# First attention and FFN of a two-layer transformer in one stage, the FFN six tiles behind

## The reference

```python
x = x + _L0_xattn_ref(_layernorm(x), ctx, ctx, Wq, bq, Wk, bk, Wv, bv, Wo, bo)   # 8 heads of 64, softmax over 64
x = x + _L0_ffn_ref(_layernorm(x), w_gate, w_up, w_down, s_gate, s_up, s_down)   # 512 -> 1376 -> 512
x = x + _L1_xattn_ref(_layernorm(x), ctx, ctx, ...)                              # linear attention
x = x + _L1_ffn_ref(_layernorm(x), W, b, A, Bmat, LiMEs)                         # low-rank experts
...
def int4_quant(x):
    beta = jnp.mean(jnp.abs(x), axis=-1, keepdims=True)
    return jnp.clip(jnp.round(x * SQRT7 / (beta + EPS)), -8, 7) * beta
def _L0_ffn_ref(x, w_gate, w_up, w_down, s_gate, s_up, s_down):
    xq = int4_quant(x)
    gate = jnp.square(jax.nn.relu(bitlinear(xq, w_gate, s_gate)))    # weights rounded to -1, 0, 1
    return bitlinear(int8_quant(bitlinear(xq, w_up, s_up) * gate), w_down, s_down)
```

## Time and profile before

| | us |
|---|---|
| median of 3 runs (757.1 to 757.83) | 757.25 |
| the profiled execution | 760.02 |
| its span, first to last instruction | 758.2 |
| busy in the span: PE | 683.5 (90%) |
| DVE | 610.3 (80%) |
| ACT | 489.1 (65%) |
| POOL | 383.5 (51%) |

### The profile page before, as it was taken

One profiled execution on the slowest core, in us unless ns is written; L12 is line 12 of the kernel. 1 busy time (PEld: TensorE's weight loads), 2 busy tenths in 40 slices (PEclk: granted clock), 3 DMA queues, 4 the chain that ended last, 5 costly groups with the idle time before them and its releaser, 6 DMA issues. The chain is left out here.

```text
span 758.2 us, 17720 instructions
## 1 busy us (share of the span) xinstructions
PE 683.5 (90%) x6622; PEld 351.3 (46%) x6649; DVE 610.3 (80%) x971; ACT 489.1 (65%) x884; POOL 383.5 (51%) x331
## 2 busy tenths in 40 slices
PE   6999999999978767599999869999999999958997
PEld 2455445454546555444444324444444444424643
DVE  6878788978745667579999868999999999958355
ACT  3888867676715666577677617878878878754320
POOL 2000009999944676432212317768777687634224
PEclk9999999999998999799999969999999999997899
DMA  5234555556334223014333200000000000025405
GB/s 169 66 127 138 201 183 146 141 155 172 82 83 130 65 68 81 10 35 78 78 69 63 65 19 1 1 2 1 1 2 1 1 2 1 1 42 109 73 1 222
DMA packets 92600, 54.71 MB, mean 72 GB/s; under 512 B 76964, under 2 KB 76964, under 8 KB 92516
## 3 DMA queue, kind: packets, MB, share of 16 engines
q1 hardware_dynamic: 91764, 53.06, 26.7%
q10 hardware_dynamic: 752, 0.52, 0.2%
HBM read 32.00 MB, written 4.19 MB: 48 GB/s over the span
## 5 line engine op out<-in xcount | busy, mean ns | idle before, releaser
L1432 POOL TENSOR_TENSOR query_qn<-query_eq,query_rq 128x1024 f32<-128x1024 f32 x64 | 122.0, 1906 | 53.3 <-DVE query_rq L1366 51.3
L684 ACT ACTIVATE keys_ek<-keys_psK,keys_mk 128x512 f32<-128x512 f32 x128 | 86.9, 684 | 40.0 <-DVE keys_mk L536 38.2
L536 DVE TENSOR_REDUCE keys_mk<-keys_psK 128x2 f32<-128x1024 f32 x64 | 78.0, 1218 | 17.2 <-PE keys_psK L743 16.9
L1357 DVE TENSOR_REDUCE query_mq<-query_psQ 128x16 bf16<-128x1024 f32 x64 | 75.5, 1180 | 4.9 <-PE query_psQ L1520 4.7
L1451 ACT ACTIVATE query_eq<-query_psQ 128x1024 f32<-128x1024 f32 x64 | 65.2, 1019 | 21.5 <-PE query_psQ L1533 21.5
L1363 DVE TENSOR_REDUCE query_lq<-query_eq 128x16 f32<-128x1024 f32 x64 | 77.3, 1207 | 2.2 <-ACT query_eq L1451 2.1
L1542 PE MATMUL query_psX<-all_ident,query_qn 128*128 128x128 f32 x512 | 70.7, 282 | 0.4 <-ACT query_qT L1458 0.4
L754 PE MATMUL keys_psT<-all_ident,keys_ek 128*128 128x128 f32 x512 | 70.8, 282 | 0.0
L766 PE MATMUL keys_psG<-keys_eT,keys_cT 128*64 128x512 f32 x256 | 69.0, 617 | 1.0 <-issue 0.9
L754 PEld LDWEIGHTS keys_psT<-all_ident,keys_ek 128*128 128x128 f32 x512 | 55.5, 142 | 28.2 <-issue 20.0
L1458 ACT ACTIVATE query_qT<-query_psX 128x1024 f32<-128x1024 f32 x64 | 65.4, 1022 | 1.1 <-PE query_psX L1542 1.1
(11 more groups left out here) (270 smaller groups left out, 1442.2 us busy)
## 6 DMA issues: line engine op xcount, KB each, us to landing
all_ring<-in_L_ffn_w_down_dram SPq DMA_DIRECT2D x8, 688.0 KB, 4.6
all_ring<-in_L_ffn_w_gate_dram SPq DMA_DIRECT2D x10, 512.0 KB, 5.4
all_ring<-in_L_ffn_w_up_dram SPq DMA_DIRECT2D x10, 512.0 KB, 4.0
all_x_res<-in_x_dram SPq DMA_DIRECT2D x4, 1024.0 KB, 6.2
att_ctx_n<-in_ctx_dram SPq DMA_DIRECT2D x16, 256.0 KB, 3.1
out_dram<-all_x_res SPq DMA_DIRECT2D x16, 256.0 KB, 2.1
all_cf<-in_ctx_dram SPq DMA_DIRECT2D x15, 256.0 KB, 2.7
att_w_nat<-in_L_ffn_W_dram SPq DMA_DIRECT2D x4, 256.0 KB, 4.4
```

The source lines that it names most:

```text
L536: dve.tensor_reduce(mk[:, c, :], psK[c % 2][:, :, :], X, ALU.max, negate=True).then_inc(mk_ok, 1)
L684: act.activation(ek[t % 2][b][:, c, :], psK[c % 2][:, b, :], ACT.Exp, bias=mk[:, c, b:b + 1], accum_out=le[t % 2][:, b, c:c + 1]).then_inc ...
L1357: dve.tensor_reduce(mq[g % 2][:, :, 0:HEADS], psQ[g % 2][:, :, :].rearrange("p b (h d) -> p b h d", d=D), X, ALU.max, negate=True).then_in ...
L1432: pool.tensor_tensor(qn[m % 2][:, :, :], eq[m % 3][:, :, :], rq[m % 2][:, :].unsqueeze(2).broadcast_to([P, 2 * HEADS, D]), ALU.mult).then_ ...
```

## The change

`attention0` and `feed_forward` become one function, `attention_and_ffn`, in one block with 25 steps. Step i handles attention tile i and FFN tile j = i - 6 (LAG), so steps 0 to 5 only attend, 6 to 15 do both, step 16 finishes tile 15 and feeds tile 10, steps 17 to 21 feed only, and 22 to 24 finish the last `down`. What else changes:

- PSUM: psWO, psV and psS give way to psA (two banks, used in turn for scores, projected, outputs and values) and psF (four: one gate bank, one for down, two for up). From j = 11 (ALONE) on, gate blocks 1 and 2 use the idle psQK banks. So several waits are new.
- Squares are made in place (three buffers r in place of r1 and r2), and the rounded h in place of hr.
- The factors are computed for two tiles at a time (GROUP), 8 times: begun in even step i, finished in i+1, inverse and products in i+2. What depends on no tile moves to `scale_constants`, before step 0.
- y = (x - mean) * s4 moves from DVE (subtract) to POOL (`scaled_x`, adding the negated mean); `quantise` on DVE keeps two operations.
- Steps that attend: quantise behind `attended(i-1)`, and SP turns h first, then a split weight, then x. Steps that only feed: quantise ahead of `gated`, SP turns x first. The test is `attends(i - 1)`.
- ACT runs `rounded(j-1)` before `heads(i+1)` while tile i attends, else behind the last square.
- Splitting of later weights moves to steps 6 to 15, the later rows to 16 to 18; the last weight and the biases are loaded into used buffers in steps 9 and 11. The three weight scales are loaded in the key stage, and its bias rows are spread two tiles later.

```diff
+        pool.tensor_scalar(k.sg[:, tiles], beta, k.ffw[:, 0:1], None, ALU.mult).then_inc(f.sc_ok, 1)
+        pool.tensor_scalar(k.su[:, tiles], beta, f.u127[:, :], None, ALU.mult).then_inc(f.sc_ok, 1)
+        pool.tensor_scalar(k.su_abs[:, tiles], beta, f.uabs[:, :], None, ALU.mult).then_inc(f.sc_ok, 1)
+        pool.tensor_scalar(k.sd[:, tiles], beta, f.down[:, :], None, ALU.mult).then_inc(f.sc_ok, 1)
+        pool.wait_ge(f.sc_ok, done + 9)
+        pool.tensor_tensor(s4, s4, rstd, ALU.mult).then_inc(f.sc_ok, 1)
+        pool.wait_ge(f.sc_ok, done + 10)
 
...
+def scaled_x(pool, k, i):
+
+    f = k.ff
+    wait(pool, f.xq_ok, i)
+    pool.tensor_scalar(f.y[:, :], k.x[:, i, :], f.nm[:, i:i + 1], k.s4[:, i:i + 1], ALU.add, ALU.mult).then_inc(f.y_ok, 1)
...
 def quantise(dve, k, i):
 
     f = k.ff
-    dve.wait_ge(f.sc_ok, 13 if i < FORE_FF else 26)
-    wait(dve, f.yr_ok, i)
-    dve.tensor_scalar(f.y[:, :], k.x[:, i, :], k.mv[:, i, 0:1], k.s4[:, i:i + 1], ALU.subtract, ALU.mult).then_inc(f.y_ok, 1)
     dve.wait_ge(f.y_ok, i + 1)
-    wait(dve, f.xq_ok, i)
-    dve.tensor_scalar(f.yr[:, :], f.y[:, :], ROUND, ROUND + 7.0, ALU.add, ALU.min).then_inc(f.yr_ok, 1)
+    dve.tensor_scalar(f.y[:, :], f.y[:, :], ROUND, ROUND + 7.0, ALU.add, ALU.min).then_inc(f.yr_ok, 1)
     dve.wait_ge(f.yr_ok, i + 1)
     wait(dve, f.xT_in[i % 2], 16 * (i // 2))
-    dve.tensor_scalar(f.xq[i % 2][:, :], f.yr[:, :], ROUND, -8.0, ALU.subtract, ALU.max).then_inc(f.xq_ok, 1)
+    dve.tensor_scalar(f.xq[i % 2][:, :], f.y[:, :], ROUND, -8.0, ALU.subtract, ALU.max).then_inc(f.xq_ok, 1)
 
...
-def attention0(nc, a, k):
+def attention_and_ffn(nc, a, k):
...
+
+        def values_at(i):
+
+            return psF[:, 2:4, LOW] if i <= LAG else psA[:, :, LOW]
+
+        def projected_at(t):
+
+            return psF[:, 0:2, LOW] if t + 1 < LAG else psA[:, :, LOW]
+
+        def outputs_at(t):
+
+            return psF[:, 0:2, HIGH] if t + 1 < LAG else psA[:, :, LOW]
+
+        def settled(i):
+
+            return i % GROUP == 0 and 0 <= i // GROUP - 2 < GROUPS
+
+        def gate_bank(j, n):
+
+            return psG if j < ALONE or n == 0 else psQK[:, n - 1, :]
+
+        def gates_free(j, n):
+
+            if j > ALONE and n == 0:
+                return NB * (j - 1) + 1
+            if j < ALONE or n == 0:
+                return NB * j + n
+            return NB * (j - 1) + n + 1 if j > ALONE else 0
 
         @block.sync
         def _(sp):
...
+            for i in range(STEPS):
+                j = i - LAG
+                if attends(i + 2):
+                    sp.wait_ge(v_ps, i + 1)
+                    load_context0(sp, a, k, i + 2)
...
+                if feeds(j + 1) and not attends(i - 1):
+                    sp.wait_ge(u_ps, NB * j)
+                    turn_x(sp, k, j + 1)
+                if feeds(j - 1):
+                    turn_h(j - 1)
+                if i == W_STEP + 3:
...
+                if i >= W_STEP + 2 and (i - W_STEP) % 2 == 0 and (i - W_STEP - 2) // 2 < NC:
+                    turn((i - W_STEP - 2) // 2)
+                if feeds(j + 1) and attends(i - 1):
+                    wait(sp, u_ps, NB * j)
+                    turn_x(sp, k, j + 1)
...
+            for i in range(STEPS):
+                j = i - LAG
+                if feeds(j + 1):
+                    scaled_x(pool, k, j + 1)
+                if feeds(j - 1):
+                    rounded(j - 1)
+                if attends(i + 2):
+                    normed(i + 2)
+                if attends(i):
+                    attention(i)
...
+            for i in range(STEPS):
+                j = i - LAG
+                if attends(i):
                     shifted(i)
...
+                if settled(i):
+                    sums_s, inverse_s, products_s = scales_of[i // GROUP - 2]
+                    inverse_s(dve)
+                if feeds(j - 3):
+                    fed(j - 3)
+                if feeds(j + 1) and not attends(i - 1):
+                    quantise(dve, k, j + 1)
+                if attends(i):
                     sums(i)
...
+                if feeds(j):
+                    gated(j, 0)
+                if feeds(j - 3):
+                    stats(j - 3, sixF, xf_ok, stf_ok, mvf_ok)
+                if attends(i - 1):
+                    attended(i - 1)
+                if feeds(j + 1) and attends(i - 1):
+                    quantise(dve, k, j + 1)
+                if attends(i - 1):
+                    stats(i - 1, sixA, xa_ok, sta_ok, mva_ok)
+                if feeds(j):
+                    gated(j, 1)
+                    gated(j, 2)
+                    scales(j)
+                if j == TILES:
+                    query_low(dve, k, 0)
...
+            for i in range(STEPS):
+                j = i - LAG
+                if finished(i):
+                    begin_x, act_x, end_x = factors[i // GROUP - 1]
+                    act_x(act)
+                if attends(i - 1) and not feeds(j):
                     projected(i - 1)
...
+                if feeds(j):
+                    gate(j, 0)
+                if attends(i):
                     exponentials(i)
...
+                if feeds(j):
+                    squared(j, 0)
+                    if attends(i - 1):
+                        projected(i - 1)
+                    if feeds(j - 1) and attends(i):
+                        rounded(j - 1)
+                if attends(i + 1):
                     heads(i + 1)
...
+                if feeds(j):
+                    gate(j, 1)
+                    squared(j, 1)
+                if attends(i + 1):
                     values(i + 1)
...
+                if feeds(j):
+                    gate(j, 2)
+                    squared(j, 2)
+                if feeds(j - 1) and not attends(i):
+                    rounded(j - 1)
+                if attends(i - 1):
+                    deviation(i - 1)
...
+                f0, f1 = FFB[n]
+                q = NB * t + n
+                if n == 0:
+                    pe.wait_ge(xT_in[t % 2], 16 * (t // 2) + 16)
+                if q == 0:
+                    pe.wait_ge(xa_ok, LAG - 1)
+                    pe.wait_ge(v_ok, LAG + 1)
+                wait(pe, r1_ok, gates_free(t, n))
+                for c in range(NC):
+                    mm = pe.matmul(gate_bank(t, n)[:, 0:f1 - f0], xT[t % 2][:, c, :], k.wgT[:, c, f0:f1], start=c == 0,
+                                   stop=c == NC - 1)
+                mm.then_inc(g_ps, 1)
+                wait(pe, h_ok, q - 1)
+                for c in range(NC):
...
+            for i in range(STEPS):
+                j = i - LAG
+                if attends(i):
                     scores(i)
...
+                if feeds(j):
+                    up(j, 0)
+                if attends(i - 1):
                     projected(i - 1)
...
+                if attends(i + 1):
                     projections(i + 1)
...
+                if attends(i - 1):
                     outputs(i - 1)
...
+                if feeds(j):
+                    up(j, 1)
+                if attends(i + 1):
                     values(i + 1)
...
+                if feeds(j):
+                    up(j, 2)
+                if feeds(j - 2):
+                    down(j - 2)
```

More of the change, by code:

```diff
@@ L35 @@
 ALL, FORE, REAR = slice(0, TILES), slice(0, TILES // 2), slice(TILES // 2, TILES)
-FORE_FF = 4
+LAG = 6
+GROUP = 2
+GROUPS = TILES // GROUP
 FF = 1376
@@ L887, in attention0 @@
-        W_STEP, ROW_STEP = 2, 2 + 2 * (NC + 1)
-        FORE_STEP = 6
-        begin_x, act_x, end_x = row_rstd(k, 1, slice(0, FORE_FF), lambda e: e.wait_ge(mv_ok, FORE_FF))
-        sums_s, inverse_s, products_s = row_scales(k, 0, slice(0, FORE_FF))
-        block = s.block()
+        dump = s.sb("dump", [P, L], BF16)
+        sixA = s.sb("sixA", [P, 6])
+        sixF = s.sb("sixF", [P, 6])
+        r = [s.sb(f"r{n}", [P, L])[:, :] for n in range(3)]
+        h = [s.sb(f"h{p}", [P, FF])[:, :] for p in range(2)]
@@ L893, in attention0, with attends, feeds, started @@
         loads = later_loads(nc, a, k)
         late_each = 4
+        block = s.block()
+        def attends(i):
+            return 0 <= i < TILES
+        def feeds(j):
+            return 0 <= j < TILES
+        def started(i):
+            return i % GROUP == 0 and 0 <= i // GROUP - 1 < GROUPS
+        def finished(i):
+            return i % GROUP == 1 and 0 <= i // GROUP - 1 < GROUPS
+        def values_at(i):
+            return psF[:, 2:4, LOW] if i <= LAG else psA[:, :, LOW]
+        def projected_at(t):
+            return psF[:, 0:2, LOW] if t + 1 < LAG else psA[:, :, LOW]
@@ L1038, in _, with rounded @@
+            def rounded(t):
+                act.wait_ge(hr_ok, t + 1)
+                wait(act, hT_in[t % 2], 16 * (t // 2))
+                act.activation(hq[t % 2][:, 0:FF], h[t % 2], ACT.Identity, bias=k.m_minus[:, :]).then_inc(hq_ok, 1)
             heads(0)
             values(0)
-            for i in range(TILES + 2):
-                if 0 <= i - 1 < TILES:
```

(7 more changed lines are left out.)

494 lines of the change are left out of this document (197 added, 297 removed).

## The result

The changed kernel takes 763.0 us (median of 20 executions, 760.4 to 766.8) against 757.95 for the kernel before, run beside it (20 executions, 755.9 to 761.3). The ratio is 1.0064, with a 95% interval of 1.0050 to 1.0078: it is slower by about 5 us. The forecast was 755.3 with faster as the likelier side. One execution of all that follow, the profiled one of f1_round_last (807.7 us at a granted clock of 0.84), was in a slower state of the chip and is left out everywhere.

What follows compares the result with a forecast made beforehand. A ring over ACT and DVE, 11.6 us, was taken to bound merged steps. 261.9 + 12.9 + 104.4 + 2.0 + 11.35 + 35.15 + 1.7 = 429.4, 2.0 under 431.39, gave 755.3 us; 8-in-10 range 748.5 to 763.5.

Steps and rivals of the forecast that it cites:

- B: Mark at the end of `down(13)`, 431.39 us before the change, forecast at 429.4, 2.0 less.
- rivals 1 and 4: Rival 1: PE's instruction-supply holes add 0.65 us to each merged step, 761.2 us, 18%. Rival 4 has its own line.
- rival 4: Cross waits make a merged step as long as its two parts, 12.5 us; 763.4 us in all, 6%.
- Step 6: First step with FFN work: x of tile 0 lands late, at 263.4, delaying the exponentials; 12.9 us.
- A: Mark at the start of tile 6's row maximum on DVE, 260.59 before the change, forecast at 261.9.
- x late in four steps: In steps 8, 10, 12, 14 weight turns precede x on SP; 0.5 us late each, 2.0 in all.
- Half speed in merged steps: PE at granted clock 0.50 after idling; the forecast charged it only behind step 16, at 1.7 us.
- The ring of 11.6: Merged steps 7 to 15: chain of ACT 7.4, DVE 2.75 and shifting 1.42 sets the step; nine steps, 104.4 us.
- PE's 10.7: PE's shorter ring in a merged step: 3.99 + 6.99, less 1.74 overlapped, plus 1.42 of shifting.
- Step 16: Passage to FFN alone: x of tile 11 lands behind h at 11.35 us, PE idle 3.4, then 1.7 at half speed.
- FFN-only steps: Steps 17 to 21: PE's 6.99 us a tile is a floor; five steps of 7.03, 35.15 us.
- The tail: Behind `down(13)`, the last two `down`, fed x and statistics: same chain in both kernels, so no difference.

Runs made afterwards that it cites:

- f1_round_last: On the three edits: ACT rounds behind the last square and SP turns x ahead of h in every step; 750.4 us.
- e2: Changed kernel with quantise of tile 0 moved in step 5 from behind attended(4) to ahead of sums(5); 757.6 us, 4.7 less than the changed kernel.
- e1: Changed kernel with x of tile 11 turned ahead of h of tile 9 in SP's step 16; 756.8 us, 5.5 less than the changed kernel.
- e3: Changed kernel with SP turning x directly behind h, ahead of loads and weight turns, in merged steps; 757.9 us, 4.4 less than the changed kernel.
- The three edits: The edits of e1, e2 and e3 together on the changed kernel; 749.5 us, and 747.2 us when run again.
- c2: On the three edits: third part of POOL's later rows moved from step 18 to 19, own bank for down(15); 747.25 us.
- c4: On the three edits: quantise behind gated block 0 in steps that only feed, step 5's staying early; 751.4 us against 747.2 for the base.
- f2: On the three edits: squares of gate blocks 0 and 1 made in three pieces each in merged steps; 749.6 us.
- c1: The kernel with the three edits and nothing else, run in two groups; 749.5 us (0.9911 of before) and 747.2 us (0.9872).
- c3: On the three edits: first quantise operation, y, put back from POOL to DVE; 749.4 us, 2.2 more than the base beside it.
- f3: On the three edits: rows' third part in step 19, own bank for down(15), and rounding last as in f1_round_last; 747.1 us, 0.9867 of before.
- e4: Changed kernel with quantise behind gated block 0 and the statistics in steps that only feed; 763.6 us, against the changed kernel's 762.3 in another group.

## Why the prediction was wrong, point by point

- **Sign.** The waits for x were seen and two holes were placed rightly; their prices were too low, and that turned a gain of 2.0 into a loss of 5. B came at 432.3 and 433.5, not at 429.4. The median lies inside the range, on the side of rivals 1 and 4, but by neither: no supply hole lengthened the merged steps of the first trace, and a merged step without a late x is 11.38, not 12.5. That 763.0 is next to rival 4's 763.4 is chance.
- **Step 6** is the step that failed most: "step 6 takes 12.9 us", measured 15.74 and 16.95. x was there for PE at 262.8 and 263.4, which looks like the predicted 263.4, but only because A came earlier. Counted from A, as the sum counts, it was issued 0.7 ahead, about as predicted (0.9), and was there 2.7 and 3.0 behind, not 1.5: it landed 3.4 and 3.2 us after its issue, not 2.4. That is 1.2 and 1.5 of the excess of 2.8 and 4.1. The rest, 1.6 and 2.6, goes with the half speed that was left out: the granted clock was 0.50 behind the wait of 3.1 to 3.5 us, as the prediction had it for step 16 alone, and in the second trace up to 268. The order gate, exponentials was right. e2 gave the whole back, 11.55; it took away wait and half speed together, so the split is worked out and not measured.
- **x late in four steps**, priced at 2.0: under-sized, and one place was denied. In the first trace PE waited 3.1 us for x in steps 11 and 12 alone (12.93 and 12.87 for 11.38 each); in e1's trace four steps (9, 11, 12 and 13) lost 5.0. e3 gave 4.4 back. "The four small loads of step 11 fit" is wrong, 1.52 us. x beside other transfers landed up to 4.5 us after its issue, where the bound had been 3.9.
- **Half speed in merged steps**, priced at nothing: 1.5 us in the first trace (step 8, 12.92), 3.0 in the second (steps 7 and 8). The three edits don't take it away: it is in c2 (steps 7 and 8), c4 (8) and f2 (8), and not in c1, c3 and f3.
- **The ring of 11.6** came out near the measured 11.38 for a wrong reason, which is luck. f1 with f3, f2 and c3 show that it has slack. The other ring was named ("`projected` waits until `shifted` ... it is in the 10.7 already") and not added up through ACT's last gate and DVE. And PE's 10.7 was below its own busy time of 10.98, which no overlap can undercut.
- **Step 16** was right: 22.43 against 23.45 for steps 15 and 16, a hole of 3.74 for 3.4. The half speed behind it came in the first trace (8.72 for a step of 7.03) and not in the second. e1 gave back 3.9 us by its trace and 5.5 by the median.
- **FFN-only steps** hold 7.03, but for step 19. The sum kept nothing for quantise first (DVE's step "just short of 7.03"); it was 1.1 us in the one step where POOL's later rows stand, and quantise behind did not take it away in c4 (8.17), though it did in e4 (7.48). The prediction hadn't followed the rows on POOL.
- **The tail**: "behind B both have the same chain" missed that one bank for `down` made `down(15)` wait 0.94 for the sum of tile 14; c2 got 0.5 back. Whether the tail lost anything against before isn't shown: from B to the query stage it is 12.61 and 12.64, and in the two traces of before 12.03 and 13.45.
- **y on POOL and the later factor chain** "worth nothing by themselves": right for the merged steps; in the steps that only feed y on POOL is worth 1.2 us by c3's trace. The factor chain alone wasn't tried.
- **A** came at 260.1 and 260.4, not 261.9: the stage began 1.8 us earlier (first maximum at 229.2, not 231.0), and steps 0 to 5 took 30.9 and 31.2 for 29.6, the 1.3 that had been forecast.
- The forecast took the profiled difference as it was. The last stage alone makes executions differ by 3 us, more than the whole forecast gain.

## What to carry to other kernels

When two stages are merged, write down for each in-order DMA queue what is issued between the last producer and the transfer that the next tile needs: here three positions in SP's and DVE's order were worth some 14 us, and putting them right turned 5 us slower into 8 to 11 faster. Price an idle stretch of PE with the half-speed work that may follow, at every place and not only at the one where the old trace shows it: here the granted clock fell behind waits of 1.8 to 3.7 us, in some executions and not in others, and in step 6 of c4 behind two of 1.36 and 0.87 us. And check each ring against the busy time of every engine on it, and follow it through shared banks: a number that fits can belong to another ring.

## What the runs showed that was not expected

- The last stage took 72.0 to 75.2 us over sixteen traces, in code that no kernel here changes. PE's granted clock, by windows over the stage, was 0.95 to 0.96 in the four traces below 73 us and 0.91 in the five of 75 and more.
- After the wait of 3.7 us ahead of `up(11)` PE ran at half speed in some executions (8.72 us for the step) and not in others (the second trace: 7.0).
- DVE's quantise operation on SBUF, begun inside POOL's rounding of h, ended 0.28 us after it every time (405.89 for 405.61, 414.00 for 413.72), 40 times over the fourteen traces of the changed kernel and its variants. Beside the POOL operations of 1.5 us on a later weight (L345, L314) 30 quantise operations began and ended inside POOL's, in 0.41 to 0.86 us, and all 28 that outlasted it again ended 0.28 after it. `gated`, which reads PSUM, wasn't held.
